# Graph-attention block with expert mixture: expert weights reach the partitions by transfers through HBM, and the gate and score steps take other places in the matmul order

## What is computed

```
logits = jnp.tanh(xt @ Wg1.T) @ Wg2.T
_, top_idx = jax.lax.top_k(logits, K)                       # K = 2 of E = 8
top_scores = jax.nn.softmax(top_logits.astype(jnp.float32), axis=1)
scores = jnp.zeros_like(logits).at[rows, top_idx].set(top_scores)
up = jnp.einsum('td,ehd->teh', xt, Wup) + bup
h = jax.nn.silu(up)
down = jnp.einsum('teh,eoh->teo', h, Wdown) + bdown
out = jnp.einsum('te,teo->to', scores, down)
```

## Time and profile before

| | |
|---|---|
| median of 3 runs | 93.64 us (93.17 to 95.05) |
| the profiled execution | 93.16 us, of which the profile's span is 91.4 us |
| busy in the span | PE 91%, weight loads 85%, DVE 71%, ACT 60%, POOL 48% |
| granted TensorE clock | 0.996 of full speed over the span |
| HBM traffic | 4.21 MB read, 1.05 MB written |
| transfers | mean 60 GB/s, nearly all in the first 16 us and for the outputs |

### The profile page before, as it was taken

One profiled execution on the slowest core, in us unless ns is written; L12 is line 12 of the kernel. 1 busy time (PEld: TensorE's weight loads), 2 busy tenths in 40 slices (PEclk: granted clock), 3 DMA queues, 4 the chain that ended last, 5 costly groups with the idle time before them and its releaser, 6 DMA issues.

```text
span 91.4 us, 1958 instructions
## 1 busy us (share of the span) xinstructions
PE 83.3 (91%) x615; PEld 78.1 (85%) x615; DVE 64.7 (71%) x202; ACT 55.2 (60%) x132; POOL 43.5 (48%) x95
## 2 busy tenths in 40 slices
PE   4959999989999999999999999999999999999800
PEld 4728888869899999989998999999999999999700
DVE  5887797857897609998599368795359767899520
ACT  1446888596695948398927799763366564433100
POOL 7970953698003999925900002885002988800000
PEclk9999999999999999999999999999999999999998
DMA  1999991000000000000000000030000030003021
GB/s 34 286 273 400 405 386 60 0 0 0 7 4 0 0 0 0 7 0 4 0 0 0 7 0 0 4 115 4 7 0 0 0 115 0 0 7 115 4 84 56
DMA packets 3339, 5.44 MB, mean 60 GB/s; under 512 B 474, under 2 KB 2748, under 8 KB 3068
## 3 DMA queue, kind: packets, MB, share of 16 engines
q1 hardware_dynamic: 3164, 5.00, 16.0%
q10 hardware_dynamic: 160, 0.26, 1.1%
HBM read 4.21 MB, written 1.05 MB: 58 GB/s over the span
## 4 chain that ended last, share of the span: by engine, by line
PE 59%; DVE 17%; DMA 6%; issue 6%; ACT 5%; DVEq 1%; POOL 1%; ACTq 1%
PE bank L734 6%; DMA ctx_sb<-in_ctx_t 6%; PE bank L735 6%; PE bank L739 6%; PE bank L896 6%; PE bank L781 5%; PE bank L872 5%; PE bank L783 5%; PE bank L782 5%; DVE hid_lo L1093 4%; PE bank L859 3%; PE bank L756 3%; DVE hid L1085 2%; PE bank L679 2%; DVE stat L990 2%
## 5 line engine op out<-in xcount | busy, mean ns | idle before, releaser
L1085 DVE TENSOR_TENSOR hid<-act_sb,bank 128x256 f32<-128x256 f32 x32 | 13.4, 418 | 10.9 <-PE bank L756 9.0
L518 ACT ACTIVATE act_sb<-bank,small_sb 128x256 f32<-128x256 f32 x32 | 15.1, 471 | 8.7 <-PE bank L739 8.4
L526 ACT CAST hid_hi<-hid 128x256 fp32r<-128x256 f32 x32 | 13.0, 405 | 10.7 <-DVE hid L1085 9.7
L781 PE MATMUL bank<-wdown_hi,hid_hi 128*128 128x256 f32 x64 | 18.4, 287 | 0.3 <-ACT hid_hi L526 0.3
L734 PE MATMUL bank<-xt_hi,wup_hi 128*128 128x256 f32 x64 | 18.0, 304 | 0.1
L783 PE MATMUL bank<-wdown_hi,hid_lo 128*128 128x256 f32 x64 | 18.1, 282 | 0.0
L782 PE MATMUL bank<-wdown_lo,hid_hi 128*128 128x256 f32 x64 | 18.0, 281 | 0.0
L735 PE MATMUL bank<-xt_hi,wup_lo 128*128 128x256 f32 x64 | 16.6, 281 | 0.0
L1093 DVE TENSOR_TENSOR hid_lo<-hid,hid_hi 128x256 fp32r<-128x256 f32 x32 | 13.4, 420 | 0.2
L739 PE MATMUL bank<-xt_lo,wup_hi 128*128 128x256 f32 x64 | 12.7, 280 | 0.0
L734 PEld LDWEIGHTS bank<-xt_hi,wup_hi 128*128 128x128 f32 x64 | 12.1, 189 | 0.5 <-ACT act_sb L518 0.3
(11 more groups left out here) (147 smaller groups left out, 180.6 us busy)
## 6 DMA issues: line engine op xcount, KB each, us to landing
x_sb<-in_x SPq DMA_DIRECT2D x4, 256.0 KB, 5.1
wup_sb<-in_wup SPq DMA_DIRECT2D x1, 1024.0 KB, 7.2
wdown_sb<-in_wdown SPq DMA_DIRECT2D x1, 1024.0 KB, 9.4
out<-out_sb SPq DMA_DIRECT2D x3, 256.0 KB, 2.2
check_sb<-in_check_w SPq DMA_DIRECT2D x1, 320.0 KB
w_sb<-in_w SPq DMA_DIRECT2D x1, 256.0 KB, 5.5
out<-out_sb SPq DMA_DIRECT2D x2, 128.0 KB, 2.5
ctx_sb<-in_ctx_t ACTq DMA_DIRECT2D x1, 192.0 KB, 5.6
```

The costliest lines, as they stand in the source:

```text
L518: nc.scalar.activation(act_out(n), bank[:, UP[n % 2], 0:N], ACT.Silu, bias=bup_sb[:, k % E:k % E + 1]).then_inc(silu_rdy, 1)
L526: nc.scalar.copy(hid_hi[:, n % HID_SLOTS, :], hid[:, n % 2, :]).then_inc(hid_hi_rdy, 1)
L781: nc.tensor.matmul(dst, hid_hi[:, n % HID_SLOTS, part], wdown_hi[:, e, :], start=False, stop=False, skip_group_check=True)
L1085: nc.vector.tensor_tensor(hid[:, n % 2, :], act_out(n), bank[:, PICK[n % 2], 0:N], ALU.mult).then_inc(hid_rdy, 1)
```

## The change

Only graph 0 keeps its picks. For graphs 1 to 3 SP writes the 256 x 8 scores of the graph to an HBM tensor as soon as POOL has made `score`, waits for that to land, and reads them back with a broadcast: each of the 128 partitions gets all 256 x 8 values, 8 KB, in all 1 MB per graph, in `score_all`. weigh then reads `score_all[:, b - 1, :, e]`, every eighth float32 of a row in SBUF, instead of the PSUM bank. In SP's queue the pairs of transfers of graphs 1 and 2 stand ahead of the store of graph 0, and that of graph 3 ahead of the store of graph 1.

gate(b) moves from step 8b to step 8b - 2, score(b) from 8b + 6 to 8b + 4; the steps of DVE and ACT between them move by as much, and the two peaks steps on PE and their DVE steps by two. weigh(8b), the first of a graph, now waits for the graph's transfer, and `dve_logits` of the next graph stands behind it on DVE.

```
-SCORE_PLACE = (3, 6, 6, 6)
+SCORE_PLACE = (3, 4, 4, 4)
...
+        score_all = sb("score_all", [P, B - 1, N, E])
+        score_hbm = [nc.dram_tensor(f"score_hbm{b}", [N, E], F32) for b in range(1, B)]
...
-        SCORE_STEPS = 9
+        SCORE_STEPS, SUM_STEP = 9, 8
...
+            def spread(run, b):
+
+                sp.wait_ge(score_step, (run * (B - 1) + b - 1) * SCORE_STEPS + SUM_STEP)
+                sp.dma_start(score_hbm[b - 1][:].rearrange("(c p) e -> p c e", p=P), score[:, pair(b), :]).then_inc(score_st[b - 1], 16)
+                sp.wait_ge(score_st[b - 1], 16 * (run + 1))
+                if run >= 1:
+                    sp.wait_ge(hid_rdy, STEPS)
+                sp.dma_start(score_all[:, b - 1, :, :], score_hbm[b - 1][:].rearrange("(a n) e -> a n e", a=1).broadcast_to([P, N, E])
+                             ).then_inc(score_all_ld[b - 1], 16)
+
             def store(run):
+                spread(run, 1)
+                spread(run, 2)
                 for b in range(B - 1):
+                    if b == 1:
+                        spread(run, 3)
                     sp.wait_ge(out_rdy, NT * run + C * (b + 1))
...
-                    if b >= 1 and e == 2:
-                        act_gate(act, run, b)
-                    if b >= 1 and e == 3:
+                    if e == 7 and b + 1 < B:
+                        act_gate(act, run, b + 1)
+                    if b >= 1 and e == 1:
                         act_diff(act, run, b)
...
-                if PICK_LAG <= i < STEPS + PICK_LAG:
+                if PICK_LAG <= i < E + PICK_LAG:
                     pe_pick(pe, run, i - PICK_LAG)
...
-                if e == 0 and 1 <= b < B:
-                    pe_gate(pe, run, b)
+                if e == 6 and b + 1 < B:
+                    pe_gate(pe, run, b + 1)
...
+                if run == 0 and i == 2 * E:
+                    pe_peaks_turn(pe)
                 if run == 0 and i == 2 * E + 2:
-                    pe_peaks_turn(pe)
-                if run == 0 and i == 2 * E + 4:
                     pe_peaks_spread(pe)
...
-            dve.wait_ge(pick_mm, n + 1)
+            b, e = k // E, k % E
+            if b == 0:
+                dve.wait_ge(pick_mm, run * E + k + 1)
+            elif e == 0:
+                dve.wait_ge(score_all_ld[b - 1], 16 * (run + 1))
...
+            weight = score_all[:, b - 1, :, e] if b else bank[:, PICK[n % 2], 0:N]
+            nc.vector.tensor_tensor(hid[:, n % 2, :], act_out(n), weight, ALU.mult).then_inc(hid_rdy, 1)
...
-                if e == 1 and 1 <= b < B:
-                    dve_gate_sum(dve, run, b)
-                if e == 2 and 1 <= b < B:
+                if e == 7 and b + 1 < B:
+                    dve_gate_sum(dve, run, b + 1)
+                if e == 0 and 1 <= b < B:
                     dve_logits(dve, run, b)
```

More of the change, by code:

```diff
@@ L221, in build @@
                              "score_step", "first_step", "score_rdy", "score_mm", "score_t_rdy"))
+        score_st, score_all_ld = ([sem(f"{n}{b}") for b in range(1, B)] for n in ("score_st", "score_all_ld"))
         up_mm, pick_mm, silu_rdy, hid_rdy, hid_hi_rdy, hid_lo_rdy, down_mm, first_half_mm, out_rdy, stored = (
@@ L746, in pe_pick @@
             if e == 0:
-                pe.wait_ge(score_t_rdy, run * B + b + 1)
+                pe.wait_ge(score_t_rdy, run * B + 1)
             if n == 0:
@@ L753, in pe_pick @@
                 pe.wait_ge(z_rdy, B)
-            if n >= 2:
+            if k >= 2:
                 pe.wait_ge(hid_rdy, n - 1)
@@ L765, in pe_down @@
                 pe.wait_ge(wdown_lo_rdy, n // EQ + 1)
+            if e == 0:
+                pe.wait_ge(score_t_rdy, nb + 1)
             if e == 0 and nb < 2:
@@ L1084, in dve_weigh @@
                 dve.wait_ge(hid_lo_rdy, n - 1)
-            nc.vector.tensor_tensor(hid[:, n % 2, :], act_out(n), bank[:, PICK[n % 2], 0:N],
-                                    ALU.mult).then_inc(hid_rdy, 1)
+            weight = score_all[:, b - 1, :, e] if b else bank[:, PICK[n % 2], 0:N]
+            nc.vector.tensor_tensor(hid[:, n % 2, :], act_out(n), weight, ALU.mult).then_inc(hid_rdy, 1)
         def dve_weigh_lo(dve, run, k):
@@ L1257, in _ @@
                                  5: [lambda: gated(3), lambda: dve_stats(dve, 0, 3)], 13: [check_peaks],
-                                 2 * E + 3: [check_peak_max], 2 * E + 5: [check_peaks_all], STEPS + 6: [check_flag]})
+                                 2 * E + 1: [check_peak_max], 2 * E + 3: [check_peaks_all], STEPS + 6: [check_flag]})
             def general():
```

## The result

The changed kernel took **103.27 us** at the median of 4 executions (101.92 to 104.29), the kernel before 93.41 beside it (93.11 to 95.05). The ratio is 1.0946, 95% interval 1.086 to 1.1031: slower by some 9%, where 94.8 us and a range of 93.0 to 97.4 had been forecast.

What follows compares the result with a forecast made beforehand. PE was taken to bound the kernel until step 31, DVE after it. weigh(24) starting 1.15 us later gave execution 93.16 + 1.15 = 94.3, and 94.8 us against the median of 93.64; range 93.0 to 97.4.

Steps and rivals of the forecast that it cites:

- the two waits of PE: PE waits some 1.2 us at score(1) for POOL's `score_parts` and 2.4 us at gate(2) for DVE's xt_lo(2).
- The picks up to up(31): 16 removed picks at steps 16 to 31, where PE bounds, at 0.117 us each: 1.9 us saved.
- I take nothing, since the row is the nearest: weigh's every-eighth read from SBUF costs nothing extra, judged by `gate_in` against `logits`, both read from PSUM.
- the upper bound of 0.27 us: One more cycle a value in weigh's read from SBUF: 256 x 1.04 = 0.27 us a weigh.
- a rival with a chance of 0.12: weigh slower from SBUF: 0.27 us on each of 8 tail pairs, 2.2 beside the 1.15, 97.0 us; chance 0.12.
- the 3.4 us from the end of up(25) to `score`: Graph 3's chain: 0.8 us to the end of `lth`, 2.58 from `prob` to the end of `score`, with handovers 3.4.
- scores 2 and 3 at 20 and 28 should find their data: PE's score(2) and score(3), at steps 20 and 28, would not wait, since no `check_peaks` stands there.
- Graph 2 had no room: Forecast that graph 2 has room: its data come at about 65, weigh(16) due with a step or two to spare.
- lateness there moves the logits of graph 3 only beyond the silu(25) that they wait for anyway: Late data for graph 2 at weigh(16) would delay graph 3's logits on DVE only within an existing wait for silu(25).
- Step 17 was put at 54.1: PE's step 17 would start at 54.1 instead of 51.04, +3.0 us, after the waits at score(1) and gate(2).
- D: Graph 3's write and read back, from `score` to weigh(24): 6.4 us taken, 6.6 with handovers; range 6.4 to 9.7, perhaps 5.

Runs made afterwards that it cites:

- The ladder: Runs from the kernel before to the changed kernel, each step changing one thing, with `check_peaks` at step 14: ratios 1.0168, 0.991, 1.0028, 1.0172, 1.0743.
- late check: The changed kernel with `check_peaks` on DVE at step 14 instead of 13, behind xt_lo of graph 2: 100.26 us, ratio 1.0743.
- filled wait: The changed kernel with 20 matmuls whose result nobody reads on PE ahead of its wait for xt_lo(2): 101.32 us, ratio 1.0897.

## Why the prediction was wrong, point by point

The ladder adds up to the whole loss. In points of ratio (1 point is 0.93 us), each the difference of two ratios above:

| from | to | points |
|---|---|---|
| before | new places, late check | +1.7 |
| | 24 picks gone | -2.6 |
| | transfer and its waits | +1.2 |
| | second operand of weigh from SBUF, adjacent | +1.4 |
| | 32-byte step | +5.7 |
| | `check_peaks` at 13: the wait at gate(2) | +2.0 |
| before | changed kernel | +9.5 |

The intervals of neighbours don't overlap, though those of the 1.2 and the 1.4 nearly touch, and each term is uncertain by a point or so. The changed kernel measured again gave 1.0837 (1.0738 to 1.0936), which would leave 0.9 for the last step and isn't told apart from the late check. The order of the steps matters too: the same early check costs 3.2 points with picks and no transfer (1.0484 against 1.0168), 4.3 with the transfer and weights from PSUM (1.0456 against 1.0028), and 2.0 at most here. That the late transfer of graph 2 hides a part of it here is argued, not tested.

Where the 32-byte step costs its 5.7 points can be read from the traces of the late check with adjacent and with spaced weights, counted from up(0) (27.19 and 25.35). The tail grows from 9.34 to 11.12 us, 1.8 us, and this is DVE's own part. up(25) comes 1.4 us later, 0.9 of it by PE's wait at score(2) for POOL. From the start of `lth` to the end of `score` of graph 3 pass 5.76 us instead of 4.21, and the transfer takes 0.2 more. Together that is 5.0 us, of which some 2.4 come through POOL's scores, more than through DVE's tail.

**What held.** One of the two waits of PE came where it was put, the other in part. up(13) started at 44.96, forecast 44.65. POOL finished `score_parts` of graph 1 at 44.71, forecast 44.4, and score(1) started at 44.77; but PE waited only some 0.4 us there, not 1.2 (the profile lists none of it, since records overlap), because it came late itself. It had waited 0.73 us at pick(3): `gate_prod` took 1.36 us instead of 0.28 while POOL worked on `wdown_lo`, so that weigh(1) came late. That wait was not forecast. xt_lo(2) cost 2.42 us at gate(2), forecast 2.4. The transfer held too: the write took 1.6 us, as taken, the read 5.24 against 4.8, and from the end of `score` to weigh(24) passed 78.88 to 85.72, 6.84 us against 6.6. The picks up to up(31) are worth 1.95 us, forecast 1.9; all 24 give 2.75 with the new places and 2.2 with the old ones.

**First failed step: the weigh from SBUF, "I take nothing, since the row is the nearest".** The row was a reduce from PSUM, and the operand in question lies in SBUF. The reading was thin besides: two rows always lie on one line, and `gate_in` takes only two values at that distance before it goes back to the neighbour of the first, where weigh steps on 256 times. Measured, the 32-byte step adds 660 - 422 = 238 ns to a weigh, 0.93 ns a value (5.7 points of the ladder with what follows from it), close to the upper bound of 0.27 us that I had put aside for a rival with a chance of 0.12. In the tail it is the rival's mechanism: from weigh(24) to the last result's first row 9.38 us became 11.16, +1.8, against the 2.2 that were worked out. The rule of the Trainium skill's page "SBUF — State Buffer" (section "Door 1: The DMA port swizzle"), that a step beyond 4 float32 pays, is what the trace shows, 660 against 422 ns; the PSUM row had no power against it.

**Second failed step, one that I didn't see: that a slower DVE is only a matter of DVE.** I costed weigh's operand on its own engine. But with `act_sb` and `score_all` both in SBUF, POOL's hits took 3.07 us for four instead of 1.73, and the scores of graph 3 needed 5.44 us instead of 2.85. Weights from PSUM bring them back to 1.8, adjacent ones from SBUF to 2.3 in one run and 2.9 in the other. So the step of the prediction that failed is the 3.4 us from the end of up(25) to `score`, of which 2.58 were taken over from the kernel before: they were 6.25 and 4.53. On the page "SBUF — State Buffer" of the Trainium skill (section "Who interferes with whom") stands that a DVE instruction with two SBUF inputs contends with a GpSimd instruction that reads SBUF; the trace agrees, 464, 634 and 711 ns a hit in the three runs. The prediction had seen DVE and POOL slow each other at `nmean` and didn't ask which new instruction would do it. The slower POOL makes the chain of scores, with the transfer behind it, the path. With it fell "scores 2 and 3 at 20 and 28 should find their data": PE waits 0.31 and 1.65 us at them for `score_parts`. Graph 2 had no room either: its data came at 71.03, forecast about 65, and weigh(16) waited 1.70 us. But "lateness there moves the logits of graph 3 only beyond the silu(25) that they wait for anyway" held, since `lth` started right behind silu(25).

**Third failed step: a wait of PE was priced by its length.** Step 17 was put at 54.1 and started at 57.69. Of the 3.6 us between, 0.4 are the later start of gate(2), 49.97 where 49.55 was taken, and some 3.2 are the half clock: 6.8 us in which PE does 3.4 us of work, and 57.94 - 54.78 = 3.16 us between the unfilled and the filled wait.

**The sum, redone for the profiled execution.** weigh(24) came at 85.72, forecast 78.3: step 17 late by 3.6, up(25) by another 0.7 (some 0.5 of it at score(2)), the scores of graph 3 by 2.6 on POOL and 0.3 in the handovers, D by 0.2: 7.4. The tail adds 1.8 and the rest 0.3; 92.55 + 9.5 = 102.1, the span. The term that the text called decisive, D, was right in size. The ladder shows that the transfer with its waits is worth only a point, since 6.8 us nearly fit between score and weigh once the scores are as quick as before.

## What to carry to other kernels

When an operand moves from PSUM to SBUF, cost it on three counts: its own step, how many SBUF inputs the instruction now has, and who on GpSimd runs beside it and feeds the path. Take the price of an access pattern from a row with the same memory, and where there is none, let the upper bound into the forecast's own case. A wait of 2.4 us in a dense PE can cost its length again in the steps behind it when the clock falls (3.2 us at step 17 here, though what of it reached the end stayed open), so first find the instruction that causes it and move that.

## What the runs showed of the hardware

- A 256-value multiply on DVE takes 418 ns with a PSUM operand, 422 with an adjacent one from SBUF and 660 with one at a step of 32 bytes.
- GpSimd's 128x8 hits take 464 ns on the mean beside multiplies with a PSUM operand, 634 with an adjacent one from SBUF and 711 with one at a step of 32 bytes.
- 8 KB from 128 partitions to HBM take 1.6 us in pieces of 32 bytes and 9.9 in pieces of 4, as two transfers; 1024 KB, the same 8 KB read for every partition, 5.2 us.
- PE idle for 2.4 us was followed by a granted clock of 0.50 for 6.8 us in three profiled executions and 3.4 us in a fourth, and not in a fifth, of the kernel without transfers. With the wait filled, none of two had such a stretch there.
